# Products of weights and values, two head pairs in every second tick, with the value projections and the reciprocals' steps in other ticks

## The reference

```python
# layer 0: causal attention with normed, rotated q and k
q = rope(rmsnorm(q, q_norm_w)); k = rope(rmsnorm(k, k_norm_w))
att = softmax(where(causal, q @ k.T / 8, -inf))      # [16 batches, 16 heads, 256, 256]
y = (att @ v) @ wo.T
# layer 1: attention with a learned bias by distance
att = softmax(q @ k.T / 8 + bias[head, bucket(k - q)])
y = (att @ v) @ o_w.T
```

## Time and profile before

| what | value |
|---|---|
| time, median of 3 runs | 2943.94 us (2940.37 to 2947.51) |
| the profiled execution, own time | 2945.17 us |
| its span | 2943.2 us |
| mean granted TensorE clock | 0.982 |
| PE / DVE / ACT / POOL busy | 95% / 72% / 58% / 35% of the span |
| DMA, mean | 64 GB/s |

### The profile page before, as it was taken

How to read it: one execution, slowest core, us unless ns; L and a number is a source line. 1 busy time by engine, 2 the same in 40 slices (tenths; PEclk the granted TensorE clock), 3 DMA queues, 4 the chain that set the end, 5 groups by cost and what they waited for, 6 DMA issues and landing times.

```text
span 2943.2 us, 68984 instructions
## 1 busy us (share of the span) xinstructions
PE 2781.4 (95%) x25484; PEld 1872.1 (64%) x25484; DVE 2119.8 (72%) x5800; ACT 1699.4 (58%) x4109; POOL 1042.9 (35%) x1420
## 2 busy tenths in 40 slices
PE   6999999989999999999999799999989988998897
PEld 2666666666666656666666455577767765666675
DVE  6988888855666566666666599746678886887674
ACT  3888888873333377777776477634325544333665
POOL 6888888821000011111111355312243330114441
PEclk9999999999999999999999899999989999999999
DMA  3111111132000011111111555200045442345750
GB/s 106 26 25 26 30 31 31 31 83 92 15 1 1 1 36 31 31 31 30 31 31 32 145 148 146 77 1 16 1 121 139 127 126 60 70 91 142 198 172 26
DMA packets 194060, 188.01 MB, mean 64 GB/s; under 512 B 14544, under 2 KB 170256, under 8 KB 192960
## 3 DMA queue, kind: packets, MB, share of 16 engines
q1 hardware_dynamic: 193728, 183.61, 24.6%
HBM read 130.24 MB, written 53.31 MB: 62 GB/s over the span
## 4 chain that ended last, share of the span: by engine, by line
PE 75%; DVE 10%; ACT 6%; issue 3%; POOL 2%; SPq 2%; DMA 1%; DVEq 0%; ACTq 0%; POOLq 0%
PE pb L160 68%; ACT big L941 4%; PE pb L637 3%; ACT big L157 2%; DVE big L2182 2%; DVE big L811 2%; PE pb L570 1%; SPq L1863 1%; PE pb L2153 1%; DMA big<-parts 1%; DVE big L231 1%; DVE big L2673 1%; PE pb L242 1%; DVE big L721 0%; DVE big L794 0%
## 5 line engine op out<-in xcount | busy, mean ns | idle before, releaser
L160 PE MATMUL pb<-big 64*128 64x256 bf16 (+12 forms) x20300 | 2522.1, 330 | 100.1 <-DVE big L2182 37.3
L160 PEld LDWEIGHTS pb<-big 128*128 128x128 f32 (+5 forms) x20300 | 1571.5, 145 | 851.1 <-issue 506.2
L157 ACT ACTIVATE big<-pb 128x512 f32<-128x512 f32 (+7 forms) x1444 | 828.3, 623 | 552.5 <-PE pb L160 313.1
L157 ACT ACTIVATE big<-pb,big 128x512 f32<-128x512 f32 (+2 forms) x536 | 315.5, 616 | 550.4 <-PE pb L160 484.3
L2182 DVE TENSOR_REDUCE big<-pb 128x4 f32<-128x1024 f32 (+1 forms) x256 | 278.4, 1087 | 81.7 <-PE pb L160 77.1
L171 POOL TENSOR_TENSOR big<-big 128x128 f32<-128x128 f32 x192 | 84.9, 456 | 654.6 <-DVE big L168 654.6
L941 ACT ACTIVATE big<-big 128x256 f32<-128x256 f32 x512 | 253.9, 498 | 68.0 <-DVE big L816 66.9
L941 ACT ACTIVATE big<-pb,big 128x128 f32<-128x128 f32 (+1 forms) x512 | 256.7, 526 | 62.3 <-DVE big L796 62.1
L811 DVE CUSTOM_DVE_ANT_0 big<-pb,big 128x256 f32<-128x256 f32 x512 | 186.6, 421 | 99.3 <-PE pb L160 99.3
L1537 DVE SCALAR_TENSOR_TENSOR big<-pb,big 128x128 f32<-128x128 f32 x512 | 144.1, 344 | 138.2 <-PE pb L160 137.4
L1020 POOL TENSOR_TENSOR big<-big 128x512 f32<-128x512 f32 x128 | 160.1, 1279 | 229.5 <-DMA big<-recip 229.3
(11 more groups left out here) (145 smaller groups left out, 2192.2 us busy)
## 6 DMA issues: line engine op xcount, KB each, us to landing
big<-parts SPq DMA_DIRECT2D x96, 512.0 KB, 4.1
parts<-big SPq DMA_DIRECT2D x384, 96.0 KB, 2.4
big<-recip SPq DMA_DIRECT2D x64, 512.0 KB, 6.8
big<-comb SPq DMA_DIRECT2D x32, 512.0 KB, 8.3
parts<-big SPq DMA_DIRECT2D x192, 64.0 KB, 2.1
big<-gates SPq DMA_DIRECT2D x8, 1024.0 KB, 6.4
big<-in_wf SPq DMA_DIRECT2D x1, 3072.0 KB, 14.8
big<-scratch SPq DMA_DIRECT2D x1, 3072.0 KB, 17.3
```

The costliest lines, as they stand in the source:

```text
L157: return e.activation(o, i, f, bias=bias, scale=scale)
L160: return e.matmul(o, l, r_, start=start, stop=stop, skip_group_check=True)
```

## The change

Values: in odd ticks from t = 3 on PE makes `value(t-3)` and `value(t-2)` one behind the other, in even ticks none. The stage has 131 ticks in place of 130. TS gets a third buffer, which lies over memory that is free in these stages, and its copies wait for a product one pair further back. The v projections and copies stand at u = 1, 3, 4, 5. The steps of the reciprocals behind the first are a tick later: transpose and spread at u = 2, scales at 4 and 5; c0 and c1 stay. In the second wide stage the negation of the maxima is made for each head by itself, and the exponentials go head by head, the second head behind a wait of its own. DVE ends a stage with a wait for the last product. Two loads for a later layer go from the head of the second wide stage to the narrow attention stage behind it, since the memory that they fill is the third TS buffer.

```diff
         EPS = alloc(64)
         WA = alloc(4096)
         WF = alloc(6400)
+        spare_at = top[0] - 256
...
             VB = [a[:, 4096:6144].rearrange("p (t h d) -> p t h d", t=2, h=16) for a in QKV]
             PS = [alloc(1024).rearrange("p (e x) -> p e x", e=2) for _ in range(2)]
             width = 384 if causal else 512
-            TS = [alloc(2 * width) for _ in range(2)]
+            TS = [alloc(2 * width) for _ in range(2)] + [WM if causal else big[:, spare_at:spare_at + 1024]]
...
             taken = [0]
             slots = {}
             hosted = not causal
-            last = 128 + 2
+            last = 128 + 3
             guests_at = 120 if causal else 112
             ahead = 2 if causal else 1
-            v_at = (2, 3, 4, 5)
+            v_at = (1, 3, 4, 5)
 
             def take(*key, ring=ring):
                 slots[key] = ring[taken[0] % len(ring)].use()
...
 
             def posts(t):
 
-                return [(step, t // 8 - 1) for step, late in (("recip", 0), ("turn", 1), ("scale0", 3), ("scale1", 4), ("c0", 6), ("c1", 7))
+                return [(step, t // 8 - 1) for step, late in (("recip", 0), ("turn", 2), ("scale0", 4), ("scale1", 5), ("c0", 6), ("c1", 7))
                         if t >= 8 and t % 8 == late]
 
             def normed_in(a):
...
             def turned_out(p, half):
 
                 n = width // 64
-                return (TS[p % 2].rearrange("p (n q) -> p n q", n=n)[:, :, 64 * half:64 * half + 64],
+                return (TS[p % 3].rearrange("p (n q) -> p n q", n=n)[:, :, 64 * half:64 * half + 64],
                         banks[2 * (p % 2) + half][:, 0:width].rearrange("p (n q) -> p n q", n=n))
 
             def value(e, p):
...
                     q0 = 128 if causal and kb else 0
                     for i in range(2):
                         t = mm(e, o[64 * i:64 * i + 64, 256 * (p % 2) + q0:256 * (p % 2) + 256], VB[b % 2][:, kb, 2 * j + i, :],
-                               TS[p % 2][:, width * i + 256 * kb:width * i + 256 * kb + 256 - q0], kb == 0, kb == 1)
+                               TS[p % 3][:, width * i + 256 * kb:width * i + 256 * kb + 256 - q0], kb == 0, kb == 1)
                 t.then_inc(pair_valued, 1)
 
             def tensor_prepare(e, t, a, b, u):
...
                         scores(e, t)
                     if 0 <= t - 1 < 128:
                         turn(e, t - 1)
-                    if 0 <= t - 2 < 128:
+                    if t >= 3 and t % 2:
+                        value(e, t - 3)
                         value(e, t - 2)
                     if 0 <= t - guests_at < guest.steps:
                         guest.tensor(e, t - guests_at)
...
                         x = slice(256 * qt, 256 * qt + 256)
                         t = e.tensor_tensor_reduce(ps[:, i, x], banks[2 * (p % 2) + i][:, x],
                                                    U[:, 2 * j + i, 128 - 128 * qt:384 - 128 * qt], 1.0, -3.0e38, ALU.add, ALU.max,
-                                                   nm[:, 2 * qt + i:2 * qt + i + 1])
-                t.then_inc(own_v.sem, own_v.up())
-                e.wait_ge(own_v.sem, own_v.n)
-                e.tensor_scalar(nm, nm, -1.0, None, ALU.mult).then_inc(pair_maxed, 1)
+                                                   nm[:, 2 * i + qt:2 * i + qt + 1])
+                    t.then_inc(own_v.sem, own_v.up())
+                    e.wait_ge(own_v.sem, own_v.n)
+                    e.tensor_scalar(nm[:, 2 * i:2 * i + 2], nm[:, 2 * i:2 * i + 2], -1.0, None, ALU.mult).then_inc(pair_maxed, 1)
 
             def ts_writable(e, p):
-                if p >= 2:
-                    e.wait_ge(pair_valued, p0 + p - 1)
+                if p >= 3:
+                    e.wait_ge(pair_valued, p0 + p - 2)
 
             def vector_prepare(e, t, a, b, u):
                 vector_project(e, a, u)
...
                     vector_squares(e, a, u)
                     if 0 <= t - guests_at < guest.steps:
                         guest.vector(e, t - guests_at)
+                e.wait_ge(pair_valued, p0 + 128)
 
             def scalar_v(e, b, n):
                 tile, half = n // 2, n % 2
...
                     norm.modulated(e, c, lambda n: HT[c % 2][:, 256 * n:256 * n + 256])
 
             def exps(e, p):
+
                 s, b, j = p % 2, p // 8, p % 8
-                e.wait_ge(pair_maxed, p0 + p + 1)
+                e.wait_ge(pair_maxed, p0 + (p + 1 if causal else 2 * p + 1))
                 if p >= 2:
                     e.wait_ge(pair_turned, p0 + p - 1)
                 if j == 0 and b >= 2:
                     e.wait_ge(recip_made, b0 + b - 1)
-                for qt in range(2):
+                for n in range(4):
+                    qt, i = (n // 2, n % 2) if causal else (n % 2, n // 2)
                     at = 0 if qt == 0 else width - 256
                     w = 128 if causal and qt == 0 else 256
-                    for i in range(2):
-                        ps = PS[s][:, i, at:at + w]
-                        m, h = 2 * qt + i, 2 * j + i
-                        t = e.activation(ps, banks[2 * s + i][:, at:at + w] if causal else ps, ACT.Exp, bias=NM[s][:, m:m + 1],
-                                         scale=rstd_q(b)[:, qt, h:h + 1] if causal else 1.0,
-                                         accum_out=SM[b % 2][:, 2 * h + qt:2 * h + qt + 1])
+                    if n == 2 and not causal:
+                        e.wait_ge(pair_maxed, p0 + 2 * p + 2)
+                    ps, h = PS[s][:, i, at:at + w], 2 * j + i
+                    t = e.activation(ps, banks[2 * s + i][:, at:at + w] if causal else ps, ACT.Exp, bias=NM[s][:, n:n + 1],
+                                     scale=rstd_q(b)[:, qt, h:h + 1] if causal else 1.0,
+                                     accum_out=SM[b % 2][:, 2 * h + qt:2 * h + qt + 1])
                 t.then_inc(pair_exped, 1)
 
             def scalar_prepare(e, t, a, b, u):
...
                 if not causal:
                     e.wait_ge(gated, 32)
                     second_gates(e, 1)
-                    e.dma_start(CT, dr["c2"]).then_inc(ld_wm, 16)
-                    e.dma_start(WM, dr["wmod2"]).then_inc(ld_wm, 16)
                 for b in range(16):
                     s = slots["turn", b]
                     e.wait_ge(s.free, s.n)
...
                           lambda e, i: hosted_step(i, lambda *at: vector_prepare(e, *at)),
                           lambda e, i: hosted_step(i, lambda *at: scalar_prepare(e, *at)),
                           lambda e, i: hosted_step(i, lambda *at: gpsimd_tick(e, *at)), nothing)
-            left = (3, 4, 6, 7)
+            left = (4, 5, 6, 7)
...
                     parts.back(e, b)
                     if k == 1 and b == 5:
                         tail.sync(e)
+                        e.dma_start(CT, dr["c2"]).then_inc(ld_wm, 16)
+                        e.dma_start(WM, dr["wmod2"]).then_inc(ld_wm, 16)
                         e.dma_start(WA[:, 0:384].bitcast(F16), dr["wa2"]).then_inc(ld_wa, 16)
                         e.dma_start(WA[:, 1152:2176], dr["rope8"]).then_inc(ld_wa, 16)
                     if k == 2 and b == 5:
```

## The result

The changed kernel takes 3056.7 us (median of 4 runs, 3046.37 to 3062.84) against 2945.73 (2940.37 to 2948.86) for the kernel before, a ratio of 1.0374 with a 95% interval of 1.0357 to 1.0391. It is slower by 111 us, where the forecast had 70 and the range ended at 3038.

A forecast was written before the change was run, and what follows sets the result against it. PE was taken as the bound (75% of the chain), with DVE, ACT and POOL close behind. First stage +25, second +42 and 1 for its first ticks, ends +2: +70 us, so 3014 us; range 2960 to 3038.

The forecast's parts named there:

- The v copy of u = 1: On DVE, ahead of the maxima, it waits for PE's values: +1.5 us a batch in the first stage, +2.4 second.
- the light ticks: Even ticks, which lose their value block but are held by the ring: 1.9 us a batch back first stage, 1.7 second.
- u=2, now 4.51, gives 0.7: First stage: tick u=2 without its value block was to shrink by 0.7 us, to 3.8.
- The clock: PE's granted clock, read as 1.00 in a stretch of the first wide stage; no term of the sum for it.
- Two negations: Second stage: splitting the negation by heads was to cost 0.1 us a batch, bounds 0 and 1.4.
- the ring through DVE's copy: Second stage: loop of turn, maxima, turned-pair copy and next scores; tick at least 3.7 us, 3.9 with two negations.
- nothing: Second stage: exponentials head by head let ACT start 0.7 us earlier, but the copy ends last, so no gain.
- The 2.11 from copy to maxima: Second stage: time from the turned-pair copy's start to the next maxima, 2.11 us, used in the 3.7 us tick minimum.
- never free: By the DVE and POOL port lock, each small negation may draw a wait, so splitting them always costs something.
- Posts a tick later: First stage: c0 on PE waits for POOL's later second scaling, +0.5 us a batch, bounds 0 and 1.0; second keeps slack.
- the rival of the pile-up: POOL's later scalings meet maxima and second negation; c0 waits 1 us or more in both stages: 3042 us, 8 in 100.
- Values in pairs: On PE, two value blocks back to back save 0.13 us a merge, 17 us in all; odd ticks +0.67 and +0.88.

The follow-up runs named there:

- experiment 4: Changed kernel with the reciprocals' transpose in tick u = 2 made six times over, to keep PE busy where it stood idle: 3033.4 us, ratio 1.0293.
- Experiment 2: Changed kernel with DVE's v copy of u = 1 placed behind the row maxima and the turned pair's copy, PE's order unchanged: 2980.1 us, ratio 1.0111.
- experiment 7: Kernel of Experiment 2 with a tick's scales ahead of its additions on POOL in the first wide stage: 2972.3 us, ratio 1.0076.
- experiment 5: Changed kernel with v steps and reciprocals' steps back in their old ticks; double value blocks, third buffer and split negation kept: 2948.0 us, ratio 0.9991.
- experiment 6: Kernel of experiment 5 with one negation for both heads instead of the split: 2966.1 us, ratio 1.0056.
- experiment 8: Kernel before, with only the negation split by heads and exponentials head by head in the second wide stage: 2935.6 us, ratio 0.9951.

## Why the prediction was right or wrong

**The v copy of u = 1** was the right main step: 6.05 and 6.86 us were forecast, and 6.15 measured in five of the first stage's twelve batches and 6.74 in the second stage at full clock (experiment 4). In five others of the first stage it was about 6.8, by the long L798 beside POOL's work; the forecast had such a hold in the light ticks and in the negations, and not here. Experiment 2 took the copy's wait away alone and gave back 77 us, where the sum had 54 for it. The difference is what the wait set off and the forecast left out.

**What followed the wait** is where the forecast failed, in "u=2, now 4.51, gives 0.7". The tick u = 2 of the first stage grew by 1.26 instead. 0.9 of the 2.0 us between the two is PE's wait for ACT's square, which I did not follow through the ring of banks; the other 1.1 is the clock. Over 14 batches that is 12 and 15 us, 27 of the 43 by which the forecast was too low. The ticks u = 1 and 2 of the second stage have 0.3 and 0.5 us a batch over their forecast, another 11 in all, and at full clock both are below it (6.74 and 3.70).

**The clock** stood in the forecast only as 1.00, as if it were given. Experiment 4 shows some 23 us for both stages together: the idle place that a wait leaves is paid a second time. PE's busy share fell to 91 and 90% in the two stages, where 94 was forecast.

**Two negations** had the wrong sign. I held the ring through DVE's copy for the one that bounds, took 0.20 for the second negation, and wrote that the earlier start of ACT brings "nothing". The ring through ACT ended last (4.05), and the split shortens it to 3.70. The 2.11 from copy to maxima was read at a place where PE was not waiting for the copy, so it was no bound; and the turn of that place waited for ACT, as the recorded rows say. The split brings 18 us with the paired values, 14 in the kernel before. That splitting them is "never free" did not come out, though DVE's small operations do get held up while POOL works: what a second negation costs now and then is less than the earlier start gives.

**Posts a tick later**: c0's wait was forecast at 0.5, bounds 0 and 1.0; its tick was 6.82 against 6.14 without, 0.7, so within them. That the later scales would meet layer norm's copies in the second stage was only in the rival of the pile-up, and was priced there as waits of 1 us at c0. It is a wait of PE at u = 4, 1.94 us in one place of the changed kernel and 2.52 in one of experiment 7. The changed kernel's u = 4 there is 4.92 in the mean, against 3.80.

**Values in pairs**: the forecast had the heavy ticks right (in experiment 5 +0.65 to +0.69 for u = 1, 3 and 5 of the first stage, against +0.67, and +0.62 to +0.86 in the second, against +0.88), the merge too (0.15 saved, 0.13 forecast), and u = 6. That the light ticks can't give all back was in the sum as well; experiments 5, 6 and 8 put the price at 12 us with the split and 16 without. So the part of the change that was meant to win loses by itself, and the only part that wins is the one that the forecast had as a small loss.

**The range** was wrong because its upper end was built only from terms that I had seen. Those that I had not (ACT's square, the clock, and POOL's work on top of DVE's in u = 1 of the first stage and u = 4 of the second) all add; the two that I had wrong the other way (negation, the ring's length) give back less.

Left open: whether k's scaling is all that holds c0's tick in experiment 7, and how the 33 us that experiment 2 leaves split up: 24 lie in the second stage, mostly in its ticks u = 4 and 5, and 7 in the first, where c0 waits.

## What to carry to other kernels

Before a step that waits is moved ahead in a tick, look at what stands behind it in its queue, and whether what it waits for is made in the same tick: here one copy moved one tick earlier cost 77 us, and moving it behind the maxima gave them back, its other place in the tick and all else the same. Follow a delay through one more round than the first: to the buffers that the late engine holds, and to the clock of an engine left idle. Of two rings that bound a tick, read each at a place where it is the one that is waited for; a distance between two rows bounds nothing if the second waited for something else. And run the parts of a change apart even where their sum is nothing: here one part cost 12 to 16 us and another won 14 to 18, and the second alone is the best kernel.

## What the runs showed of the hardware

An idle place of PE of 1.6 us with one of 0.6 behind it (312.74 and 314.39 of the changed kernel) was followed by some 6 us at half clock, though PE is busy 91% of the stage; idle places of 0.86, 0.59 and 0.87 us (190.08, 191.71 and 193.17) were not, and the clock stayed at 1.00. Five needless transposes in that place made the kernel 23 us faster. Two DVE operations that take 0.60 us together took 2.31 while POOL worked on long tensor operations, in a stage where POOL is busy only 17% of the time (experiment 7); and one DVE operation on 4 columns took 0.87 where 0.16 is usual, under a single POOL operation of 1.04, and ended with it.
